# Turning queries and keys at the head of each step of a software pipeline on TensorE

## The reference

```
for i in range(6):
    x = attn_layer(shift_tokens(x), ...) + x     # 16 heads of 64, windows of 32 tokens
    x = ffn_layer(shift_tokens(x), ...) + x
# attn_layer
q, k = l2norm(q) * qs, l2norm(k) * ksc
q = q * cos * scale + rotate_half(q) * sin * scale     # k likewise, with 1 / scale
out = local_attention(q, k, v)                         # own window and the one before it
return out.reshape(...) @ Wo
```

## Time and profile before

| | |
|---|---|
| time before, median of 3 runs | 4850.1 us (4849.73 to 4854.78) |
| profiled execution, its own time | 4845.42 us |
| its span, first to last instruction | 4843.6 us |
| granted TensorE clock, mean | 0.955 |
| busy over the span: TensorE, weight loads, VectorE, ScalarE, GpSimd | 88%, 61%, 61%, 58%, 64% |
| steps of a stack | 192, in two stacks: about 401 to 2089 us and 2244 to 3931 us |

### The profile page before, as it was taken

The page is one execution under the profiler, slowest core; times in us unless marked ns, Lnnn a source line. Parts: engine busy times, 40 slices in busy tenths (PEclk is TensorE's granted clock), DMA queues, the critical chain, the costliest instruction groups (busy, mean ns, idle before and its releaser), DMA issues.

```text
span 4843.6 us, 164846 instructions
## 1 busy us (share of the span) xinstructions
PE 4281.7 (88%) x66235; PEld 2961.0 (61%) x66235; DVE 2953.1 (61%) x5388; ACT 2789.5 (58%) x6175; POOL 3089.8 (64%) x1906
## 2 busy tenths in 40 slices
PE   7898999999999999977999999999999972769985
PEld 4565666666666666645666666666666641535554
DVE  5665666666666666735666676666666645245551
ACT  4555666666666666644666666666666641335552
POOL 1117888888888888825888888788887835121102
PEclk9999999999999999989999999999999985879997
DMA  2002333333333333311333333333333310300004
GB/s 64 0 0 74 90 106 95 99 97 91 104 89 108 89 101 95 90 46 55 90 108 93 96 104 86 106 91 101 98 93 102 88 43 0 106 13 0 0 1 124
DMA packets 349769, 367.30 MB, mean 76 GB/s; under 512 B 58737, under 2 KB 285042, under 8 KB 348786
## 3 DMA queue, kind: packets, MB, share of 16 engines
q1 hardware_dynamic: 338834, 348.92, 25.3%
q0 software_dynamic: 2048, 4.20, 0.3%
q10 hardware_dynamic: 8160, 3.93, 0.3%
HBM read 247.13 MB, written 109.71 MB: 74 GB/s over the span
## 4 chain that ended last, share of the span: by engine, by line
PE 33%; ACT 8%; issue 4%; DVE 3%; POOL 2%; SPq 2%; DMA 1%; ACTq 0%; DVEq 0%; POOLq 0%
PE banks L327 5%; PE banks L388 3%; PE banks L311 3%; PE banks L332 2%; PE banks L859 2%; PE banks L829 2%; PE banks L432 2%; PE banks L371 2%; PE banks L294 2%; PE banks L426 1%; ACT arena L463 1%; PE banks L1192 1%; PE banks L1212 1%; PE banks L842 1%; ACT ln_rs L469 1%
## 5 line engine op out<-in xcount | busy, mean ns | idle before, releaser
L639 POOL TENSOR_TENSOR arena<-arena 128x512 f32<-128x512 f32 x768 | 959.9, 1271 | 520.0 <-DVE arena L568 396.4
L644 POOL TENSOR_TENSOR arena<-arena 128x1024 f32<-128x1024 f32 x384 | 905.0, 2357 | 30.1
L641 POOL TENSOR_TENSOR arena<-arena 128x1024 f32<-128x1024 f32 x384 | 907.7, 2364 | 0.0
L327 PE MATMUL banks<-w_qk,arena 128*128 128x512 f32 x1536 | 738.0, 604 | 16.3 <-DVE arena L668 10.6
L442 ACT COPY arena<-banks 128x512 f32<-128x512 f32 x384 | 223.9, 583 | 799.6 <-PE banks L388 799.6
L568 DVE SCALAR_TENSOR_TENSOR arena<-arena,banks 128x512 f32<-128x512 f32 x768 | 493.6, 684 | 309.9 <-ACT arena L476 308.4
L561 DVE TENSOR_REDUCE arena<-arena 128x8 f32<-128x512 f32 x768 | 494.3, 679 | 84.5 <-ACT arena L458 83.9
L535 DVE TENSOR_REDUCE arena<-banks 128x8 f32<-128x512 f32 x384 | 265.0, 690 | 394.2 <-PE banks L311 390.0
L458 ACT ACTIVATE arena<-banks 128x512 f32<-128x512 f32 x768 | 446.7, 595 | 85.4 <-PE banks L327 73.4
L1006 POOL TENSOR_TENSOR arena<-arena,hmask 128x1024 f32<-128x1024 f32 x64 | 120.1, 1907 | 568.7 <-ACT arena L878 309.8
L327 PEld LDWEIGHTS banks<-w_qk,arena 128*128 128x128 f32 x1536 | 278.3, 194 | 274.0 <-issue 274.0
(11 more groups left out here) (204 smaller groups left out, 7745.7 us busy)
## 6 DMA issues: line engine op xcount, KB each, us to landing
v_rows<-arena SPq DMA_DIRECT2D x1536, 64.0 KB
arena<-v_rows SPq DMA_DIRECT2D x768, 128.0 KB, 2.6
arena<-v_rows SPq DMA_DIRECT2D x768, 112.0 KB, 2.4
arena<-in_moe_w SPq DMA_DIRECT2D x30, 515.5 KB, 3.8
w_qk<-in_stack_qk SPq DMA_DIRECT2D x48, 256.0 KB, 3.1
w_v<-in_stack_v SPq DMA_DIRECT2D x48, 128.0 KB, 3.4
w_o<-in_stack_o SPq DMA_DIRECT2D x12, 512.0 KB
w_w<-in_stack_w SPq DMA_DIRECT2D x12, 341.0 KB, 3.2
```

What stands on the lines that cost most here:

```text
L327: pe.matmul(bank(M, tile), f.sh[:, (s // G) % 2, o:o + 128], w.qk[:, g], start=True, stop=True).then_inc(S.qk, 1)
L639: nc.gpsimd.tensor_tensor(f.sined[:, :, :, half, :], x[:, :, :, 1 - half, :], sines[:, :, mine].unsqueeze(1).to_broadcast([D, GH, 4, DH // ...
L641: nc.gpsimd.tensor_tensor(rot, x.rearrange("p h t a d -> p h t (a d)"), cosines.unsqueeze(1).to_broadcast([D, GH, 4, DH]), ALU.mult).then_ ...
L644: nc.gpsimd.tensor_tensor(rot, rot, f.sined.rearrange("p h t a d -> p h t (a d)"), ALU.add).then_inc(S.rotated, 1)
```

## The change

In `pe_stack_step` the two calls of `pe_stack_heads` move from behind the outputs to the head of the step, ahead of mask, scores and outputs. No other engine's list is changed.

```
     pe, s, S, f, w = st.eng, st.s, M.st, stack_buffers(M), M.w
     y = bank(M, 7, T)
+    if st.on(2):
+        pe_stack_heads(M, st, 0)
+        pe_stack_heads(M, st, 1)
     if st.on(3):
         u = s - 3
         st.wait(S.heads_taken, u + 1)
...
         last.then_inc(S.outs, 1)
-    if st.on(2):
-        pe_stack_heads(M, st, 0)
-        pe_stack_heads(M, st, 1)
     pe_stack_hidden(M, st, 0)
```

## The result

The changed kernel takes 5086.09 us (median of 4 runs, 5080.65 to 5089.81), the kernel before 4852.44 us in the same session: ratio 1.0478, 95% interval 1.046 to 1.0496. The forecast was 5067, the range 4955 to 5120.

A forecast was written before the change was run, and what follows sets the result against it. TensorE, 88% busy, was taken to bound the kernel. Terms 1.8 + 2.75 - 0.2 + 0.6 - 0.3 = +4.65 us a pair, times 47 = 219 us on 4845.42, gave 5068, rounded to 5067; range 4955 to 5120.

The forecast's parts named there:

- Two links close a loop over two steps: Rotated unit asked for 1.85 us sooner and finished later; heads, outputs, VectorE, GpSimd, heads two steps on: 17.4 and 17.6 us.
- Steps 4 and 5: Loop of 17.6 us against 14.88 us now: +2.75 us a pair, less 0.1 for ScalarE's earlier exponential.
- The wait for bank 3: TensorE stands 1.2 us at the head of step 5 until ScalarE takes the turned outputs; part of the 2.75 us.
- Steps 0 and 1: Loop of 17.4 us against 15.59 us now: +1.8 us a pair, less 0.1 for ScalarE's earlier exponential.
- Steps 2, 3, 6 and 7: Too long for the loop to bind; L371 waits add 0.6 us a pair, step 6's shorter L311 wait takes off 0.3.
- The gain: Outputs start 0.93 us later in the step, so most of the L482 wait goes: at most 52.5 us, 1.1 a pair.
- The second: Rival: VectorE's and GpSimd's work hangs on the projections, not the outputs' end; +2.3 us a pair, 4958 us; chance 0.10.
- the first: Rival: the two-step loop through VectorE and GpSimd sets the pace, clock held; 5068 us, own range 5020 to 5125; chance 0.68.
- The third: Rival: TensorE's clock falls once a pair, +0.9 to +1.8 us a pair, 5110 to 5153 us; chance 0.10.
- The fourth: Rival: new waits only displace TensorE's old idle time of 3.3 us a pair; +1.3 a pair, 4911 us; chance 0.06.
- The fifth: Rival: the rotated unit is there anyway, so only the L482 wait goes; faster, 4798 us; chance 0.04.
- the sixth: Rival: nothing measurable, gain and loss equal at 1 us a pair; loops would be 3.6 us a pair shorter; chance 0.02.

The follow-up runs named there:

- keys first: Changed kernel with keys turned and copied ahead of queries, so the bank 3 wait stands four transposes later: 5095.93 us, ratio 1.0497.
- Taking the loop away: Changed kernel with GpSimd's last operation on a unit (L644, adds the sine part) left out: 4990.44 us, ratio 1.0278.
- the early wait: Kernel before, order unchanged, plus a wait at each step's head for ScalarE's copy of the turned outputs (bank 3): 4868.2 us, ratio 1.0035.
- the keys alone: Changed kernel with only the keys' transposes put back between scores and outputs, queries staying at the step's head: 5111.29 us, ratio 1.0537.

## Why the prediction was right

*Two links close a loop over two steps.* Right. L388 starts 0.06 us behind GpSimd's end in steps 2 and 6, and the distance from the issue of the outputs' successor to GpSimd's end is 1106.06 - 1091.31 = 14.75 us in step 4 (14.80 less 0.1 predicted). With the heads between scores and outputs the wait on GpSimd was half as long; a shorter unit of GpSimd took it away. The profile sign was over-sized, however: some 80 us of waiting for L644 from 400 to 2000 us were named, and there are 48.1, since other delays (bank 3, "issue", TensorE's own longer work) fill part of the loop.

*Steps 4 and 5.* +2.78 us, +2.65 predicted. The wait for bank 3 at the head of step 5 lay inside, as the prediction had it; keys first shows it. Step 4 with it lasts 8.34 us in the pair shown (8.3 predicted), but the wait itself is 0.54 us, not 1.2: the rest of the step has grown by 0.7 us, 0.25 of it a wait of a feed-forward piece for ScalarE.

*Steps 0 and 1.* +0.93 in the mean, +1.7 predicted: over-sized. The distance to GpSimd's end was 1143.68 - 1129.83 = 13.85 us, not 14.1, since the exponential no longer stands behind two copies. Of the 0.35 us kept for the wait on L482 almost nothing is left: 1129.83 - 1126.95 = 2.88 us from the head to the projections, against 2.78 without a wait. And the mean of the kernel before (16.28) is longer than the pair that was read (15.59), because of the gaps of "issue" and the slow stretches in step 0 where a new layer begins. In step 0 those gaps come to 22.6 us before and 17.6 after; in step 1 they rise from 1.7 to 25.0.

*Steps 2, 3, 6 and 7.* +1.1 us, +0.3 predicted: under-sized. The projection L371 waits 55.6 us instead of 38.7, 0.2 a time, near the 0.3 taken. What was missing is "issue", 31 us more in these four steps, 0.65 a pair (step 2 went from 8.87 to 9.50 us in the mean), and the change of form: the transposes ahead of the mask save 0.03 to 0.06 us a step, the projections right behind the outputs lose 0.10. "Nothing is added" had put both at nothing. So two sizes were off by about as much in opposite directions, and the nearness of 5067 to 5086 owes something to that.

*The gain.* It was there: 51 us of waiting at the outputs vanished. The loop and the rest cost nearly six times as much.

*The rivals.* The second (all hangs on the projections) gave 16.45 and 16.7 us for the loops; measured 16.79 in the pair shown and 17.5. In steps 0 and 1 it was nearer than the first. The distance that it held fixed, from L327 to GpSimd's end, went from 13.27 to 13.85 and from 13.87 to 14.75 us; the first's went from 14.20 to 13.85 and from 14.80 to 14.75. The third fell: the clock is 0.957, where it was 0.955. But the evidence against it was read too strongly. The 1.00 from 400 to 2000 us is a rounded mean, and the kernel before does fall to half clock behind gaps that are each under 2 us, as the lines of step 0 above show. The rule that the prediction quotes speaks of long gaps; the prediction stretched it to waits of 1.2 to 2 us. The fourth fell: TensorE's idle time grew by 190 us. The fifth fell: L388 waits 159.5 us. In the sixth the 3.6 us are a slip: the sum of 4.65 us a pair already has the gain in it, so the loops would have to be shorter by 4.65.

*What the prediction didn't say*: how much of the cost would stay if GpSimd were faster. It spoke of a wait inside the loop and stopped there. Taking the loop away returned 79 us; bank 3, gaps, the later projections and TensorE's longer busy time held the other 145.

*The gaps of "issue".* They come at places that repeat from layer to layer, sit mostly inside the blocks of small matmuls, and appear when the transposes stand ahead of the scores in all steps (99 us after; 96 without L644; 103 with keys first). They are 27 us with the heads between scores and outputs, 36 with step 0 alone in front, 47 with the early wait. Neither the wait on GpSimd nor the one on bank 3 makes them. What TensorE waits for there can be read from the trace's records of single transfers. The page of the changed kernel names a DMA queue for instructions:

```profile
...
q8 instruction: 524, 8.59, 0.7%
...
```

These are 524 transfers of 16,384 bytes, 509 of them in the stacks, one for about 250 of TensorE's instructions. In the stacks of the changed kernel there are 94 gaps of "issue" over 0.3 us, and every one ends 1.17 to 1.83 us after the end of such a transfer; before there are 28, and every one ends 1.24 to 1.99 us after one. Stretches between 1.1 and 2.0 us behind a transfer's end make up only an eighth of the time, so this is no accident. TensorE stands because its next instructions come late. The gap shown above, in step 7, ends at 1118.64; the transfer ran from 1116.06 to 1117.42. From the start of a transfer to the end of the gap it takes about 2.6 us in the median, and scores and outputs together, 128 matmuls and 128 weight loads, are about one transfer's worth used up in 1.55 us. A pause between the two would then shorten the gaps, and they are 27 us with the whole heads there and 72 with the keys alone.

*Open*: why the supply is late three times as often in the one order as in the other. No run moves the block's place among the transfers by itself.

Not tried: VectorE's maximum released by the scores alone, which would shorten the loop by 0.78 us. It would read a bank while TensorE writes the outputs to it.

## What to carry to other kernels

Before a consumer is moved up in a software pipeline, take the margin of its latest producer against the new place, step by step, and add what the move delays on the producer's own side: here 1.85 us sooner and 0.93 us later met a margin of 0.56 to 0.85 us. A wait that reads as almost zero in the list says nothing of that margin. The move paid in the one step where there was something to gain and the producer was early enough even for the new place (the unit turned in step 0 was done at 1003.87 us, 2.1 us before the step's start), and a second limit can lie just behind the one that the profile names, so take the first away in an experiment before pricing a cure. Compare busy times too: an order can cost through longer work and late instructions where no engine is waited for.

## What the runs showed of the hardware

- Going from 64 x 32 matmuls back to full 128 x 128 ones cost TensorE 0.05 to 0.15 us each time (four transposes 0.44 and 0.59 us; eight transposes 0.87 and 0.93, and 1.02 with small matmuls on both sides; projections 1.72 and 1.82 us).
- Two waits of 1.3 to 1.6 us on TensorE in each 76 us left the granted clock near its upper level of 2.4 GHz in the stack: 0.99 from 400 to 2000 us, 1.00 from 2400 to 4000 us, and 0.957 over the whole span, against 0.955 before. But gaps of that size did sometimes bring it down: 0.73 and 1.94 us with 0.7 us of work between them in the kernel before, at 932 to 935 us, and one of 1.54 us in the changed kernel, which ended at 1491.29 us. Behind both the projections took 2.60 us instead of 1.72. Most gaps of 1 to 2 us were not followed by it.
- Gaps of 0.3 to 2.5 us of "issue", most of them inside blocks of small matmuls, changed from 36 to 99 us in all by order alone, with the same instructions. Each ended 1.1 to 2.2 us after the end of a 16,384-byte transfer of the instruction queue, in all 630 cases over 0.3 us in the eleven kernels' stacks.
